# One cross product instead of two in the routing Gram matrix of a two-layer attention and expert kernel, with a doubled copy of the high half

## The reference

```python
h = jax.nn.relu(jnp.einsum('btd,edh->ebth', x, Wd1) + bd1[:, None, None, :])
recon = jnp.einsum('ebth,ehd->ebtd', h, Wd2) + bd2[:, None, None, :]
losses = jnp.mean((recon - x[None]) ** 2, axis=(2, 3))
idx = jnp.argmin(losses, axis=0)
```

## Time and profile before

| | |
|---|---|
| median of 3 runs | 2355.91 us (2355.46 to 2357.37) |
| the profiled execution | 2356.12 us, of which the span of the trace is 2354.4 us |
| PE, DVE, ACT, POOL busy | 89%, 63%, 40%, 29% of the span |
| mean clock granted to PE | 0.979 of full speed |
| Gram matmuls (L1090), 128 x 128 | 1536, 219 ns median each, 233.3 us busy |
| Gram matmuls (L1090), 128 x 257 | 1536, 273 ns median each, 260.9 us busy |
| low half of H on DVE (L1522) | 128, 684 ns mean, 87.5 us busy |

### The profile page before, as it was taken

One profiled execution on the slowest core, in us unless ns is written; L12 is line 12 of the kernel. 1 busy time (PEld: TensorE's weight loads), 2 busy tenths in 40 slices (PEclk: granted clock), 3 DMA queues, 4 the chain that ended last, 5 costly groups with the idle time before them and its releaser, 6 DMA issues.

```text
span 2354.4 us, 60990 instructions
## 1 busy us (share of the span) xinstructions
PE 2091.9 (89%) x26095; PEld 1366.3 (58%) x26095; DVE 1480.7 (63%) x3341; ACT 930.2 (40%) x1618; POOL 675.1 (29%) x902
## 2 busy tenths in 40 slices
PE   1589999989999999999999999999999999999955
PEld 1264755647475565747556574756657475665724
DVE  5366667675766667576676757666675766666531
ACT  1234344353434435344443534434353443435220
POOL 2113132231513233151322315132231514223051
PEclk9989999999999999999999999999999999999978
DMA  3322121131412113141211314121131412112010
GB/s 79 92 48 72 30 76 44 25 103 29 109 29 75 44 22 107 29 108 29 77 43 31 98 29 109 29 79 41 32 96 29 109 29 82 40 38 71 11 36 18
DMA packets 166422, 134.06 MB, mean 57 GB/s; under 512 B 86476, under 2 KB 137173, under 8 KB 166135
## 3 DMA queue, kind: packets, MB, share of 16 engines
q1 hardware_dynamic: 166152, 130.17, 22.4%
HBM read 36.99 MB, written 16.78 MB: 23 GB/s over the span
## 4 chain that ended last, share of the span: by engine, by line
PE 66%; DVE 13%; SPq 8%; ACT 5%; issue 4%; POOL 2%; DMA 1%; DVEq 1%; POOLq 0%; ACTq 0%
PE NS L874 11%; PE ringF L1090 10%; SPq L394 8%; PE ringF L1075 7%; PE ringA L778 7%; PE KV L955 5%; PE ringA L1041 5%; PE ringF L1123 3%; PE ringA L917 3%; DVE stage L1511 3%; PE ringA L941 2%; PE ringF L778 2%; PE ringF L1125 2%; ACT E L638 2%; PE ringF L1071 2%
## 5 line engine op out<-in xcount | busy, mean ns | idle before, releaser
L1090 PE MATMUL ringF<-x,H 128*128 128x257 f16 x1536 | 260.9, 273 | 0.0
L1435 DVE TENSOR_REDUCE mx<-ringA 128x8 f32<-128x512 f32 x256 | 175.3, 685 | 115.4 <-PE ringA L917 115.3
L1090 PE MATMUL ringF<-H 128*128 128x128 f16 x1536 | 233.3, 220 | 1.4 <-DVE H L1522 1.4
L630 ACT ACTIVATE E<-ringA,score_scale 128x512 f32<-128x512 f32 x256 | 175.2, 686 | 119.1 <-PE ringA L941 119.1
L778 PE MATMUL ringA<-xT,wqkv 128*128 128x512 f16 x768 | 179.3, 384 | 30.5 <-DMA KS<-KS 14.0
L1488 DVE SCALAR_TENSOR_TENSOR X<-X,NS 128x320 f32<-128x320 f32 x160 | 77.9, 487 | 180.8 <-PE NS L874 175.7
L1075 PE MATMUL ringF<-wd,x2T 128*128 128x512 f16 x768 | 189.6, 383 | 0.0
L638 ACT ACTIVATE E<-ringA,score_scale 128x512 f32<-128x512 f32 x256 | 158.6, 684 | 76.1 <-PE ringA L972 76.1
L450 POOL TENSOR_SCALAR vtmp<-mv,eps_ffn 128x8 f32<-128x8 f32 x16 | 5.1, 316 | 626.0 <-DVE mv L1267 626.0
L1421 DVE TENSOR_REDUCE mx<-ringA 128x1 f32<-128x512 f32 x256 | 161.6, 682 | 26.8 <-PE ringA L908 25.6
L450 POOL TENSOR_SCALAR vtmp<-mv,eps_ln 128x8 f32<-128x8 f32 x32 | 10.0, 314 | 577.1 <-DVE mv L1267 563.2
(11 more groups left out here) (248 smaller groups left out, 4494.4 us busy)
## 6 DMA issues: line engine op xcount, KB each, us to landing
KS<-stage SPq DMA_DIRECT2D x384, 64.0 KB, 2.0
QS<-stage SPq DMA_DIRECT2D x384, 64.0 KB, 2.0
xin<-in_L_attn_x_dram SPq DMA_DIRECT2D x16, 1024.0 KB, 10.9
xres<-in_L_attn_x_dram SPq DMA_DIRECT2D x16, 1024.0 KB, 8.0
out_dram<-yout SPq DMA_DIRECT2D x16, 1024.0 KB, 5.5
QS<-LB SPq DMA_DIRECT2D x16, 512.0 KB, 4.4
E<-in_L_attn_w_qkv_dram SPq DMA_DIRECT2D x1, 768.0 KB
E<-in_L_ffn_Wd_dram SPq DMA_DIRECT2D x2, 256.0 KB
```

Of the source, the lines that this page charges most:

```text
L630: A(E[:, k % ESLOTS, :], ps[:, :], ACT.Exp, scale=score_scale[:, 0:1]).then_inc(freed["s3"].sem, 1)
L1090: ins = MM(dst, H[:, a, t, own], src, start=first and i == 0, stop=last and i >= 4, skip_group_check=True)
L1435: V_.reduce_max(mx1[:, t, 8 * h:8 * h + 8], take(b, "m1", k)[:, :].rearrange("p (a m) -> p a m", a=8), AX.X)\
```

## The change

`H` gets a third plane, `H[:, 2, t, :]`, which holds twice the high half. DVE makes it, right behind the low half of the same tile, and signals a new semaphore `h2`. The Gram product then takes low.T (2 high) in place of high.T low + low.T high. The two differ as matrices (one is the transpose of the other's first term), but they are multiplied by a symmetric block and summed, which gives the same number. The product of a pair and a tile has five matmuls instead of six.

```diff
-        H = sb("H", [P, 2, T, EH], F16)
+        H = sb("H", [P, 3, T, EH], F16)
...
             def gram(b, q, tiles):
                 if q == 0 and 0 in tiles:
                     pe.wait_ge(freed["h"].sem, freed["h"].at(b, T))
+                    pe.wait_ge(h2.sem, h2.at(b, T))
...
-                            (0, ps[:, 0:P], H[:, 0, t, own]), (0, ps[:, 0:P], H[:, 1, t, own]),
+                            (0, ps[:, 0:P], H[:, 0, t, own]),
                             (0, ps[:, P:GR], x16[:, 0, t, 0:C + 1]), (0, ps[:, P:GR], x16[:, 1, t, 0:C + 1]),
-                            (1, ps[:, 0:P], H[:, 0, t, own]), (1, ps[:, P:GR], x16[:, 0, t, 0:C + 1]))):
-                        ins = MM(dst, H[:, a, t, own], src, start=first and i == 0, stop=last and i >= 4, skip_group_check=True)
+                            (1, ps[:, 0:P], H[:, 2, t, own]), (1, ps[:, P:GR], x16[:, 0, t, 0:C + 1]))):
+                        ins = MM(dst, H[:, a, t, own], src, start=first and i == 0, stop=last and i >= 3, skip_group_check=True)
...
                 V_.scalar_tensor_tensor(out=H[:, 1, t, :], in0=bank("h", t)[:, :], scalar=0.0, in1=H[:, 0, t, :],
                                         op0=ALU.max, op1=ALU.subtract).then_inc(freed["h"].sem, 1)
+                V_.tensor_scalar(H[:, 2, t, :], H[:, 0, t, :], 2.0, None, ALU.mult).then_inc(h2.sem, 1)
```

## The result

| | median | runs |
|---|---|---|
| before | 2355.68 us | 4, from 2353.48 to 2357.37 |
| changed | 2338.88 us | 4, from 2336.27 to 2343.32 |

The ratio is 0.9931, with a 95% interval from 0.9913 to 0.995: 16.8 us or 0.7% faster. The forecast was 2336.0 with 2330 to 2346, so 20 us. The direction holds, and three to five of the twenty microseconds are missing. What became of them is the question of this part.

The account below looks back on a forecast made before the run. Bound by a chain of stacking DMAs, PE and DVE turns over maxima, then PE's Gram product. 25.8 us from removed matmuls less 5.8 for doublings gives 20.0 off 2356.12, forecast 2336.0 us, range 2330 to 2346.

Parts of the forecast that it names:

- The bound: Three stretches per batch: stacking DMAs, then PE and DVE taking turns over maxima, then the Gram product straight through PE.
- 0.057 us per removed matmul, 28 per batch and 32 in the tail: Gram product on PE: 452 removed matmuls on the path over 15 batches and tail, 25.8 us gained.
- The four of the first half: Removed matmuls in pair 0's first Gram half, each batch: worth nothing, PE would only wait longer for DVE's transposed operand.
- A doubling at four elements per cycle, 0.21 us to the next instruction: Added DVE instruction, 128 x 512 float16: 0.30 us long, next start after 0.21 us, bounds 0.14 and 0.60.
- The rival of half or full length: Doubling on DVE followed after 0.34 or 0.60 us instead of 0.21: time 2340.1 or 2348.2; chance 0.10.
- 0.16 + 0.21 us at maxima 4 and 9: Delays behind the doublings of tiles 4 and 7 on DVE: 0.37 us per batch, 5.6 us over 15 batches.
- The tail's wait: In the tail PE's Gram product now waits for the last doubling too: 0.21 us.
- The cover: Gram halves hiding DVE's and ACT's iteration turns: smallest slack 1.09 us, 0.23 needed; rival of too little slack 2360.1, chance 0.03.
- The clock: PE's falls to half clock in the stacking stretch: none to eight batches instead of four, about 4 us either way.
- The rival that had the clock fall in the Gram stretch: PE's longer wait at 1227 tips the clock in each batch: 21 us lost, 2352 to 2361; chance 0.05.

Follow-up runs that it names:

- the thin one: The changed kernel with only two of the five Gram products per token tile (high.T high and high.T x-high): 2234.78 us, 104 us under the changed kernel.

## Why the prediction was right, and what it had mis-sized

- **The bound.** Right. Stacking DMAs, maxima, Gram product on PE: the chain of the changed kernel has the same three stretches.
- **0.057 us per removed matmul, 28 per batch and 32 in the tail.** Right: 1.57 us per batch measured against 1.60, 1.80 us in the tail against 1.82.
- **The four of the first half are worth nothing.** Right: the wait grew by their 0.23 us, and the time stayed the same.
- **A doubling at four elements per cycle, 0.21 us to the next instruction.** Right: 0.28 us long, 0.20 us apart. The rival of half or full length is out.
- **0.16 + 0.21 us at maxima 4 and 9.** Right: 0.37 and 0.38 us per batch in two comparisons, 0.15 by `scores3(5)` and 0.37 by `scores3(10)`, and none when the doublings are moved. Only the sign was wrong: the forecast wanted the 0.16 us as a wait at k = 5, and the profile shows it as a later start without idle time.
- **The tail's wait.** 0.26 us instead of 0.21, a trifle.
- **The cover.** The slack was enough for the change, as forecast. But the slack as I had read it, 1.09 us in ACT's copies, was not the one that gives out first; it bore 0.23 + 1.11 us without a wait. The one that does has a POOL instruction in it, which already stretched DVE's L1468 to 0.82 us in the kernel before.
- **The clock.** Here lies the shortfall. I had named the falls, placed them rightly in the stacking stretch, and allowed none to eight of them, centred on the four of before. They came in 12 and in 9 batches of two profiled executions. By the means of the table a fall goes with 0.7 to 0.85 us more in the changed kernel, so five to eight more of them are 3.5 to 7 us. The measured shortfall is 3.2 to 4.7 us. The mis-sized term is the number of falls: none to eight allowed, 12 and 9 counted. Their price was put loosely too. The two batches of the earlier trace rows are 137.96 - 136.41 = 1.55 us apart and not 1.4, and 136.41 is shorter than the usual 136.68; in the mean a fall goes with 0.79 us in the kernel before. So four falls more or fewer are 3 us and not "about 4". The time stayed inside the range although the number of falls did not, because the other terms came out almost exactly and the room kept for them was not needed. The rival that had the clock fall in the Gram stretch did not happen: no fall lies there.

## What to carry to other kernels

Price a removed matmul by the distance between starts, and count only those that stand in the chain of waits: here 28 of 32 per batch counted, and the other four bought nothing. An added instruction on an engine that is nearly the bound costs only where a reader waits behind it, and the cost can hide in the distance between two starts where no idle time shows. Moving the same instruction by a few places brought back all it had cost. And a kernel that is made shorter in one stretch can change how often PE's clock falls in another, so look at the granted clock of both profiles before the difference is put down to the edit.

## What the runs showed of the hardware that I had not expected

- PE's clock fell after stretches in which its longest single wait was short: 2.49 us before one of the twelve falls of the changed kernel, and 0.75 to 1.53 us before the eleven others (longest wait in the 16 us ahead of each). This is the longest:

```profile
1176.28 0.99 PE L909 MATMUL ringA<-KS,QlB 96*128 96x512 f16 x3 [2.49 <-DVE stage L1372]
```

- Six useless matmuls per batch, about 1.3 us of PE's work in its idle time, took the falls from 9 batches in 14 to 2 and made the changed kernel 3.3 us faster. In the kernel before, the same matmuls from the third batch on left 3 falls of 4 and brought nothing.
- A POOL instruction on two SBUF operands held a DVE instruction with two SBUF inputs up: 2.15 us instead of 0.69. The busy time of all 80 of them was 59.0 us in the kernel before (mean 738 ns), 62.2 us in the changed one (778 ns) and 77.6 us in the thin one (970 ns). It was there before the change, hidden by the Gram halves. In all three it ended 0.54 to 0.56 us after the POOL instruction.
- POOL needed 1.49 us to double a 128 x 512 float16 tile, five times as long as DVE's 0.28 us.
